# The opening of an attention and FFN kernel: context tiles ahead of the positions, K's low part between gathers, x's statistics behind the context's low parts

## The reference

```python
x = x + _L0_xattn_ref(_layernorm(x), ctx_4096, ctx_4096, pos, mask, Wq, Wk, Wv, Wo)
x = x + _L0_ffn_ref(_layernorm(x), weight, bias, gate_w, in_channel_scale, out_channel_scale)

def _L0_xattn_ref(query, key, value, position_ids, src_mask, Wq, Wk, Wv, Wo):   # 32 heads, 8 KV heads, D = 128
    q, k, v = heads(query @ Wq), heads(key @ Wk), heads(value @ Wv)
    cos, sin = cos_t[position_ids], sin_t[position_ids]
    q = q * cos + _rotate_half(q) * sin
    k = k * cos + _rotate_half(k) * sin
    scores = where(mask == 0, -1e9, q k^T / sqrt(D))
    return (softmax(scores) @ v) @ Wo

def _L0_ffn_ref(x, weight, bias, gate_w, in_channel_scale, out_channel_scale):
    routing = softmax(x @ gate_w.T)
    return x * (routing @ in_channel_scale) @ sign(weight).T * (routing @ out_channel_scale) + bias
```

## Time and profile before

| | us |
|---|---|
| median of 3 runs (1177.56 to 1177.73) | 1177.7 |
| the profiled execution | 1177.43 |
| its span, first to last instruction | 1175.6 |
| TensorE busy (share of the span) | 1159.1 (99%) |
| VectorE busy | 802.8 (68%) |
| GpSimd busy | 707.3 (60%) |
| ScalarE busy | 552.3 (47%) |

### The profile page before, as it was taken

How to read it: one execution, slowest core, us unless ns; L and a number is a source line. 1 busy time by engine, 2 the same in 40 slices (tenths; PEclk the granted TensorE clock), 3 DMA queues, 4 the chain that set the end, 5 groups by cost and what they waited for, 6 DMA issues and landing times.

```text
span 1175.6 us, 23824 instructions
## 1 busy us (share of the span) xinstructions
PE 1159.1 (99%) x7684; PEld 953.9 (81%) x7684; DVE 802.8 (68%) x1359; ACT 552.3 (47%) x1768; POOL 707.3 (60%) x589
## 2 busy tenths in 40 slices
PE   8999999999999999999999999999999999999996
PEld 7788888888888888888888888888888888888875
DVE  6876676676676666677676666776667676666664
ACT  4554454445544354454444453544444354444442
POOL 5755566655557665566655576655567565676525
PEclk9999999999999999999999999999999999999997
DMA  8322433233223223343322232332333222222200
GB/s 237 99 87 85 119 120 98 66 95 105 77 73 107 72 79 97 96 112 107 99 75 71 82 107 78 91 104 78 87 100 90 63 80 65 86 90 82 71 1 37
DMA packets 136348, 104.99 MB, mean 89 GB/s; under 512 B 12712, under 2 KB 111016, under 8 KB 136288
## 3 DMA queue, kind: packets, MB, share of 16 engines
q1 hardware_dynamic: 128848, 93.72, 27.5%
q10 hardware_dynamic: 6672, 8.40, 2.2%
q0 software_dynamic: 768, 2.10, 0.6%
HBM read 100.00 MB, written 4.19 MB: 89 GB/s over the span
## 4 chain that ended last, share of the span: by engine, by line
PE 95%; DVE 1%; POOL 1%; ACT 1%; issue 1%; DMA 1%; POOLq 0%; ACTq 0%; DVEq 0%
PE chunk L1133 25%; PE chunk L1134 24%; PE chunk L1135 24%; PE o_ps L1206 5%; PE sc_ps L1181 3%; PE tr_ps L1181 2%; PE aux L1122 2%; PE o_ps L1122 2%; PE tr_ps L1122 1%; PE sc_ps L1122 1%; PE aux L1286 1%; PE aux L1287 1%; PE aux L1260 1%; DMA qT<-in_ctx 1%; PE aux L1272 0%
## 5 line engine op out<-in xcount | busy, mean ns | idle before, releaser
L422 POOL TENSOR_TENSOR w_lo<-raw,w_hi 128x512 fp32r<-128x512 f32 x192 | 247.3, 1300 | 373.7 <-ACT w_hi L548 373.6
L876 DVE TENSOR_TENSOR swp<-chunk,sinT 64x512 f32<-64x512 f32 x320 | 220.3, 688 | 99.4 <-PE chunk L1135 95.3
L1133 PE MATMUL chunk<-xT_hi,w_hi 128*128 128x512 f32 (+1 forms) x512 | 208.9, 408 | 0.6 <-POOL w_lo L422 0.6
L1134 PE MATMUL chunk<-xT_lo,w_hi 128*128 128x512 f32 (+1 forms) x512 | 200.8, 392 | 0.0
L1135 PE MATMUL chunk<-xT_hi,w_lo 128*128 128x512 f32 (+1 forms) x512 | 200.1, 391 | 0.0
L1133 PE MATMUL chunk<-wo_hi,oT_hi 128*128 128x512 f32 x496 | 196.8, 397 | 1.2 <-POOL wo_lo L422 0.8
L1135 PE MATMUL chunk<-wo_hi,oT_lo 128*128 128x512 f32 x496 | 193.7, 390 | 0.0
L1134 PE MATMUL chunk<-wo_lo,oT_hi 128*128 128x512 f32 x496 | 193.2, 390 | 0.0
L429 POOL TENSOR_TENSOR qT<-qT,swp 128x512 f32<-128x512 f32 x128 | 167.2, 1306 | 40.0 <-DVE qT L878 38.0
L584 ACT ACTIVATE probs<-scores,neg_max 128x64 f32<-128x64 f32 x512 | 170.4, 335 | 27.3 <-DVE neg_max L833 27.3
L818 DVE TENSOR_TENSOR acc<-chunk,acc 128x512 f32 (+1 forms) x128 | 88.2, 689 | 137.3 <-PE chunk L1135 136.8
(11 more groups left out here) (281 smaller groups left out, 1907.9 us busy)
## 6 DMA issues: line engine op xcount, KB each, us to landing
raw<-in_L_xattn_Wq SPq DMA_DIRECT2D x128, 256.0 KB, 2.8
raw<-in_L_xattn_Wo SPq DMA_DIRECT2D x128, 256.0 KB, 2.7
raw<-in_L_xattn_Wk SPq DMA_DIRECT2D x32, 256.0 KB, 4.6
raw<-in_L_xattn_Wv SPq DMA_DIRECT2D x32, 256.0 KB, 3.0
acc<-in_x ACTq DMA_DIRECT2D x14, 256.0 KB, 2.9
c_tile<-in_ctx SPq DMA_DIRECT2D x12, 256.0 KB, 2.9
x_tile<-in_x SPq DMA_DIRECT2D x12, 256.0 KB, 3.4
result<-y ACTq DMA_DIRECT2D x12, 256.0 KB, 2.0
```

The costliest lines, as they stand in the source:

```text
L422: nc.gpsimd.tensor_tensor(lo, raw[:, r, :], hi.bitcast(F32), ALU.subtract).then_inc(wsplit_lo, 1)
L876: last = nc.vector.tensor_tensor(swp[to, k, :], bank[of, :], sinT[to, here], ALU.mult)
L1133: nc.tensor.matmul(bank, a_hi, b_hi, start=i == 0, stop=False)
L1134: nc.tensor.matmul(bank, a_hi, b_lo, start=False, stop=False)
```

## The change

ACT issues context tiles 2 and 3 first and the positions behind them. DVE works on the positions after `cT_lo` of tile 0, and on the statistics of x tiles 0 and 1 after all four `cT_lo` instead of between them. POOL makes K's low part after the second gather, no longer after the fourth.

```diff
--- before.py
+++ after.py
@@ -529,7 +529,8 @@
                 wait_alone(pool, pos_first_ok, 1)
                 for p in range(PAIRS):
                     gather_rows(rows_first[:, p, :], pos_first[:, p:p + 1]).then_inc(rows_first_in, 16)
-                split_lo(first, 0)
+                    if p == 1:
+                        split_lo(first, 0)
                 split_lo(first, 1)
                 pool.wait_ge(consts, 1)
                 pool.wait_ge(x_st3, PAIRS)
@@ -792,10 +793,10 @@
                     scaled(cosT[:, bass.ts(i, 2 * P)], ROWS_BANK[i][:, 0:2 * P])
                     scaled(sinT[:, bass.ts(i, 2 * P)], ROWS_BANK[i][:, 2 * P:4 * P]).then_inc(rope_ok, 2)
 
+            for p in (2, 3):
+                nc.scalar.dma_start(c_first[:, p, :], row_of(ctx_t, p)).then_inc(c_first_in[p], 16)
             nc.scalar.dma_start(pos_i[:, :], pos.rearrange("(n b) s -> (b s) n", b=2),
                                 allow_slow_non_contiguous=True).then_inc(pos_in, 16)
-            for p in (2, 3):
-                nc.scalar.dma_start(c_first[:, p, :], row_of(ctx_t, p)).then_inc(c_first_in[p], 16)
             for p in (2, 3):
                 nc.scalar.dma_start(acc[:, p, :], row_of(x_t, p)).then_inc(x_first_in[p], 16)
             first_slot = Slot(0, 0, False, False)
@@ -1083,13 +1084,14 @@
                     dve.wait_ge(x_first_in[p], 16)
                     nc.vector.bn_stats(s_stat[:, p, :], acc[:, p, :]).then_inc(x_st1, 1)
 
-                first_positions()
                 for p in range(PAIRS):
                     dve.wait_ge(c_hi, p + 1)
                     here = bass.ts(p, P)
                     lo_of(cT_lo[:, :, here], by_chunk(C_BANK[p]), cT_hi[:, :, here]).then_inc(c_lo, 1)
-                    if p == 1 or p == 2:
-                        stats_of(p - 1)
+                    if p == 0:
+                        first_positions()
+                stats_of(0)
+                stats_of(1)
                 stats_of(2)
                 stats_of(3)
                 for p in range(PAIRS):
```

## The result

The changed kernel takes 1183.62 us in the median of 5 runs (1183.36 to 1184.09), the kernel before 1177.73 (1177.56 to 1178.3). The ratio is 1.005 with an interval of 1.0035 to 1.0064: 5.9 us slower, where 1.9 were forecast and 3.5 was the end of the range. The profiled execution took 1183.85 us, 6.42 more than that of before.

What follows compares the result with a forecast made beforehand. GpSimd's order and its holding off VectorE were taken to set when TensorE can begin x's transposes. The later cast, +2.17, less 0.31 from GpSimd's new order, gave +1.86 us: 1179.6 against 1177.7, range 1177.4 to 1181.2.

Steps and rivals of the forecast that it cites:

- What bounds the opening: Opening: GpSimd sets the pace by its order and by holding VectorE off twice; 7.35 us from first gather to s_rstd.
- The cast at 7.63, behind the first cT_lo: VectorE's first step on the positions starts at 7.63 at best instead of 5.46: +2.17 us.
- the positions' own packets need one to two and a half us more beside wk: 6.0 to 7.5: ScalarE's queue: positions land at 6.0 to 7.5, before the cast's 7.63; upper end 8.9, adding 1.27 us.
- late positions: Rival, chance 0.30: positions land after 7.63, each 0.1 us moving the end 0.1; 1180.4 in the middle, 1180.8 at most.
- The order of these changes while their number doesn't: ScalarE's DMA issues: table load stays at 5.01 to 6.29 and the first cT_hi at 6.31.
- K's low part between the gathers, -0.31 us: GpSimd, first gather to s_rstd: 7.34 us in the new order instead of 7.66, 0.01 on top: -0.31 us.
- K's earlier projection: TensorE: K's projection starts 0.34 us earlier, worth nothing since TensorE then waits for x anyway.
- x's statistics, at nothing: VectorE: statistics behind the context's low parts cost nothing, under GpSimd's 3 us; without that cover at most 1.3 us.
- The clock: Rival, chance 0.05: TensorE's idle times lower its granted clock in the opening, costing 3 us or more: 1182.6.
- The shift of x's transposes is the shift of the end: TensorE has no gap after x's transposes, so their shift, +1.86 us, moves the end equally.
- the end's low stretch falls otherwise: Rival, chance 0.09: the later program avoids the clock's fall near the end and gets back 3.2 us: 1176.4.
- The gathers' landing: Last gather lands at 18.8 to 21.1, TensorE wants it at 21.26: costs nothing; chance 0.04 of over 21.3.

Runs made afterwards that it cites:

- Experiment 9: Changed kernel, first four tiles' positions (512 pieces) first on ScalarE and VectorE, rest behind x tiles, s_rstd and x's normalization before V's low part: 1175.89 us, repeated 1176.33.
- experiment 1: Changed kernel with only ScalarE's issue order undone, positions ahead of context tiles 2 and 3: 1179.6 us, ratio 1.0018.
- Experiment 3: Changed kernel, where SyncE waits for the positions before issuing what follows Wk (x tiles 0 and 1, Wv, Wq): 1179.88 us, measured once.
- experiment 4: Changed kernel with positions in two transfers, 512 pieces where all 2048 were, the other 1536 behind x tiles 2 and 3: 1180.19 us, ratio 1.0021.
- experiment 6: Kernel before the change with only K's low part moved between the gathers: 1177.65 us, ratio 1.0002.
- experiment 2: Kernel before the change with only ScalarE's issue order changed, positions behind context tiles 2 and 3: 1185.87 us, ratio 1.0072.
- experiment 7: Kernel before the change with only x's first two statistics moved behind the context's low parts: 1177.7 us, ratio 1.0002.
- experiment 5: Changed kernel with the positions last on ScalarE's queue, behind x tiles 2 and 3 as well: 1184.88 us, measured once.

## Why the prediction was wrong

- **What bounds the opening** (GpSimd's unbroken row of work from the first gather to s_rstd, and VectorE held off twice): right. 7.32 us of it were measured, 7.35 forecast, and x_tile took 1.49 us again. Experiment 9 shows it by taking V's low part away: s_var and x_tile are short, and x comes 2.3 us earlier.
- **The cast at 7.63, behind the first cT_lo**: right only with the positions first (7.47 in experiment 1). In the changed kernel 12.30. **This is the step that failed**: "the positions' own packets need one to two and a half us more beside wk: 6.0 to 7.5", and its upper end, 8.9, from a context tile's landing. Experiments 3 and 4 show what was in its place: the positions' 2048 pieces need 2.1 us when SyncE's queue holds back, and some 6.3 us beside its traffic, and with 512 pieces they land 3.7 us earlier. The landing was at 12.3, the term 6.8 us instead of 2.2. The kernel's text gives the number of pieces; I bounded the cost by bytes and by a transfer of large pieces.
- **What the 7 packets in the earlier trace rows meant**: I read them as a gap that the positions might meet, and gave "late positions" 0.30. The case had the right sign and the wrong mechanism, and its price ended at 3.1 us. From 8 to 9 us the two queues moved as many pieces as each other (437 and 438), and such a share helps the queue with few large pieces and holds up the one with many small ones. The rule that I cited from the Trainium skill (DMA: Bandwidth & Descriptors, "Queues, rings and completion order"), turns between the queues, was nearer to what happened than the gap was; I drew the wrong conclusion from it. The even counts fit it; whether a turn is one piece or an equal group of them no run here tells, and the 332 to 64 from 6.5 to 7.0 us it doesn't explain.
- **"The order of these changes while their number doesn't"**, for ScalarE's issues: wrong. The two behind the positions took 4.98 us instead of 2.50 and pushed the first cT_hi to 8.48. It cost nothing here, since the positions came 2.50 us later still. Experiment 3 shows that it comes next once the positions are earlier: there the cast waits for cT_lo, at 9.37.
- **K's low part between the gathers, -0.31 us**: right in the changed kernel (0.34), where s_var is long done. In experiment 6, where s_var is still held off, it is 0.06 (7.60 us from the first gather to s_rstd instead of 7.66). What I costed at nothing, K's earlier projection, is worth something once the positions are late: without it K's projection holds x by 1.4 us (experiment 2).
- **x's statistics, at nothing**: right (experiment 7).
- **The clock**, 0.05 at 3 us: the granted clock did fall, between 13.4 and 15.1 us in the changed kernel, after TensorE had stood still. It cost nothing, since x was later still. In experiments 6 and 7 it fell in the opening too, and K's projection then held x by 0.2 and 0.4 us.
- **The shift of x's transposes is the shift of the end**: right within 0.1 us for the profiled pair (6.49 and 6.4), but by two errors of 0.4 us that cancel. In experiment 3 they don't: x's transposes are 3.56 us late (21.10), the product ahead of the idle time near the end 2.98 (1150.67), the end 2.4 (1178.0). In experiment 4 it is 2.91, 2.71 and 2.4. A part comes back near 549 us, as said above, and a part in the stretch at the lower clock: the rival "the end's low stretch falls otherwise" (0.09) was at work, at a sixth of its 3.2 us. Behind this list are its rows.
- **The gathers' landing**: named with 0.04, and seen in experiments 1 and 9 as waits of 0.79 and 0.94 us. (The prediction's own terms put the last gather at 14.52, not 14.45, which changes nothing.)

The windows of the earlier trace rows, moved along with the work, for the changed kernel and for experiment 3:

```profile
1154.05:1157.35 3.30, 0.00 (x0) 0.00 (x0) 1.96 (x8) 0.53 (x3) 1.99 (x3) 1.00 0.01 2
```

```profile
1150.98:1154.28 3.30, 0.00 (x0) 0.00 (x0) 1.96 (x8) 0.53 (x3) 1.99 (x3) 0.74 0.01 2
```

TensorE stands idle in this window, so a lower clock costs nothing in it, and what follows is work. Its granted clock there is 0.92 in the kernel before. In the changed kernel it is 1.00, and the time from there to the end is 0.4 us longer than before. In experiment 4 it is 0.82 and the time 0.3 us shorter, in experiment 3 it is 0.74 and the time 0.6 us shorter. So differences of half a microsecond between two kernels can come from where the clock falls and not from the change.

What stays open is why ScalarE's two issues behind the positions take 4.6 to 5 us when two tiles stand ahead of the positions and 2.5 us when none does. That it goes with the number of pieces is shown (1.11 us with 512), not what is full. Open too is what the idle time of 0.40 us at 549 us is, which some of the kernels have and others don't, and what sets the two queues' shares outside the stretch from 8 to 9 us.

## What to carry to other kernels

Ask of each small transfer how many pieces it has and what else is in flight when its turn comes: thousands of single elements have to go while the other queues are empty, or be cut to what is needed first, and neither their bytes nor their issue time say when they land. Where one engine's row of work sets the pace, look also at what it holds off on its neighbour: with V's low part away from around s_rstd, x came 2.3 us earlier, where moving the loads brought 0.84. About half of that was lost at once to the next wait.

## What the runs showed of the hardware

- The same 8 KB transfer of 2048 pieces landed 4.7 us after its issue at the head of the program, 6.1 us with the other queue held back, 10.6 beside a busy queue, and 11.4 when issued 1 us later still, behind two more tiles. In 1 us of the stretch in which it was slow the two queues moved 437 and 438 packets; in another half us it was 64 and 332.
- The two DMA issues behind it on the same engine took up to 5 us, where they take 0.99 without it ahead (experiment 5), and what stands behind that on the engine's own stream is late too; here it was ScalarE's table load, of 1.28 us.
- s_var, four columns wide, takes 0.17 us, and 0.41 to 1.43 where it meets one of GpSimd's low parts; x_tile takes 0.55 and 1.49 to 1.52. The Trainium skill (SBUF — State Buffer, "Who interferes with whom") has the rule: VectorE in certain forms and GpSimd need the same pair of ports, and the one that comes second stands still until the other's instruction ends. The trace agrees, by these durations: s_var ends within 0.1 us of the low part's end, wherever it started. x_tile ends 0.28 us behind it, a little sooner than the 0.55 it takes alone. Not all forms are held off: each of x's four statistics takes 0.67 to 0.68 us in the kernel before and in the changed one, beside a low part or not.
